# Perceiver block on one core: key rows by SBUF-to-SBUF transfers, batch 0 prepared alone, squarings moved, and key scores and exponential per head

## Chip, cores and metric

One core of a Trainium2 chip runs the whole program in one launch. The metric is device microseconds of that core, median of three runs. All matrix data are float32 or, where the text says so, bfloat16 (bf16).

## What is computed

The reference is one Perceiver layer on x (4 batches, 128 tokens, 128 features) and a context of 2048 rows per batch; attention has 16 heads of 8 features:

```python
q = (layernorm(x) @ Wq.T + bq);  k = ctx @ Wk.T + bk;  v = ctx @ Wv.T + bv      # per head: 8 columns
attn = softmax(q @ k.T / sqrt(8) + mask)                                        # 128 x 2048 per head
x = x + (attn @ v) @ Wo.T + bo
sigma = svd(W)[0];  W_in, W_out = W / max(sigma, 1)                             # largest singular values
x = x + gated_scan(layernorm(x), W_in, W_out, Wp, ...)                          # 128 steps
x = x + (gelu(layernorm(x) @ bw1.T + b1) @ bw2.T + b2)                          # bw: alpha * sign(w)
```

## The kernel before

**Units.** Attention runs over 4 batches x 8 pairs of heads x 4 chunks of 512 keys = 128 units. For each unit TensorE makes three products. `scores` (L418) is queries x keys, 128 x 512 for each head of the pair, in bf16: the two heads lie in partitions 0 to 63 and 64 to 127 of `k_rows`, so each of the two matmuls uses one half of the array's rows. VectorE takes the row maximum of it (`pmax`, L1191). Then `keyscores` (L434) makes the same product the other way round, keys x queries, with the maximum subtracted: 8 matmuls of 128 keys x 128 queries, four for each head, and in the kernel before the heads alternate (j outside, head inside). ScalarE takes the exponential of both heads in one instruction (`probs`, L739), and `pv` (L447) multiplies with the values, 16 float32 passes onto four column groups.

**Splitting.** A float32 query or key is held as three bf16 parts; the contraction of a head is over 8 features x 6 products of parts = 48 rows, plus 3 rows for the maximum in `keyscores`.

**Key rows.** The three parts lie feature by feature in `k_parts`. To get the 48 rows of a head, SP stores each chunk to DRAM (`store_k`, L259, three DMAs of 384, 256 and 128 KB) and loads two blocks of 192 KB for each pair (`load_pair`, L267) into one of four slots of `k_rows`. Queries go the same way, once (`q_rows_dram`, L282 and L288). GpSimd copies the query block and the value block of each pair (`q_now` L982, `v_now` L959).

**Order.** Chunks 0 to 7 (batches 0 and 1) are turned, projected and split before attention starts. Then the loop over g = 0 to 127 issues on TensorE, in this order, `keyscores(g + 1)`, `scores(g + 8)`, `pv(g)` and one piece of side work:

```python
keyscores(g + 1); scores(g + LEAD); pv(g)        # LEAD = 8
if g < 64:    side_prep(8 + g // 8, g % 8, i)    # one of chunks 8 to 15 per 8 units
elif g < 112: side_squares(g, i)                 # 3 squarings per 8 units
else:         side_last(g, i)
```

Of 8 units in `side_prep` one turns the context chunk (L320), two project halves of K (L487), two halves of V (L495), two (g % 4 == 1) turn the running output and the next maximum (`side_turns`, L455 and L460), and one has no side work. The largest singular values come from 24 squarings of a Gram matrix: six lie in the preparation, 18 in `side_squares`. All waits are on semaphores written by hand: `keyscores(g + 1)` waits for the exponential of g, the exponential of g + 1 for `keyscores(g + 1)`, since there is one pair of PSUM banks (4 and 5) for it; `scores(u)` waits for the maximum of u - 2. `side_prep(8, 0)` waits for context chunk 8. TensorE, ScalarE, VectorE, GpSimd and SP's queue each execute in the order of the program.

Of the kernel before, what the change touches and what calls it, by code (L numbers as in the profile page):

```python
# [43 lines left out]
def perceiver_block(nc, x, ctx_in, mask, Wq, bq, Wk, bk, Wv, bv, Wo, bo, W_in, W_out, Wp, bp,  # L44
# [25 lines left out]
    HALF_ROWS = 64  # L70
    LOADS = 32
# [4 lines left out]
    with ctx:  # L76
# [41 lines left out]
        q_now = sb("q_now", [P, 4, T], BF16)  # L118
        ctx_buf = sb("ctx_buf", [P, FIRST, 4, D])
        ctxT = sb("ctxT", [P, 2, 512])  # L120
        k_parts = sb("k_parts", [P, 3, B * KEYS], BF16)
        k_r1 = sb("k_r1", [P, 2, 512])
        k_32 = sb("k_32", [P, 2, 512])
# [3 lines left out]
        v_now = sb("v_now", [P, 2, KT, 2 * HEAD_COLS])  # L127
# [8 lines left out]
        o_nat = w1_nat  # L136
# [26 lines left out]

        q_dram = nc.dram_tensor("q_rows_dram", (D, BLOCKS, TOK), BF16, kind="Internal").ap()
        k_dram = nc.dram_tensor("k_rows_dram", (B, D, BLOCKS, KEYS), BF16, kind="Internal").ap()

        ld = {n: sem("ld_" + n) for n in ("ident", "x", "kv", "vec_qk", "vec", "ssm", "w", "mlp",
                                          "mask", "rows")}  # L170
        ctx_loaded = [sem(f"ctx_loaded{c}") for c in range(FIRST)]
# [14 lines left out]
        k_stored_first = sem("k_stored_first")  # L186
        k_stored_rest = sem("k_stored_rest")
        q_now_ready = sem("q_now_ready")
        k_rows_loaded = [sem(f"k_rows_loaded{s}") for s in range(4)]
        v_now_ready = sem("v_now_ready")  # L190
# [40 lines left out]

        @block.sync
        def _(sp):
            def load_ctx(n):
                wait(sp, ctx_turned, n - FIRST + 1)
                b, c = divmod(n, CHUNKS)
                sp.dma_start(ctx_buf[:, n % FIRST, :, :], ctx_in[b, 512 * c:512 * c + 512, :].rearrange(
                    "(p j) d -> p j d", j=4)).then_inc(ctx_loaded[n % FIRST], 16)

            sp.dma_start(w_kv[:, 0, :], Wk).then_inc(ld["kv"], 16)  # L240
            load_ctx(0)
            sp.dma_start(w_kv[:, 1, :], Wv).then_inc(ld["kv"], 16)
            sp.dma_start(w_kv[:, 2, :], Wq).then_inc(ld["kv"], 16)
            load_ctx(1)
            sp.dma_start(w_nat[:, W_IN, :], W_in).then_inc(ld["ssm"], 16)
            sp.dma_start(w_nat[:, W_OUT, :], W_out).then_inc(ld["ssm"], 16)
            for n in range(2, FIRST):
                load_ctx(n)
            sp.dma_start(mask_sb[:, :], mask.rearrange("a b q k -> (a b q) k")).then_inc(ld["mask"], 16)
            sp.dma_start(w1_nat[:, :, :], w1.rearrange("(a p) d -> p a d", p=P)).then_inc(ld["mlp"], 16)  # L250
            sp.dma_start(w2_nat[:, :], w2).then_inc(ld["mlp"], 16)


            def store_k(n):
                b, c = divmod(n, CHUNKS)
                sp.wait_ge(k3_ready, n + 1)
                keys = slice(512 * c, 512 * c + 512)
                for first, parts in K_GROUPS:
                    sp.dma_start(k_dram[b, :, first:first + parts, keys],  # L259
                                 k_parts[:, 0:parts, 512 * n:512 * n + 512]  # L260
                                 ).then_inc(k_stored_rest if b else k_stored_first, 16)

            def load_pair(i):
                b, p = divmod(i, PAIRS)
                wait(sp, keyscores_ready, CHUNKS * (i - 3))
                for h in range(2):
                    sp.dma_start(k_rows[HALF_ROWS * h:HALF_ROWS * h + ROWS, i % 4, :],  # L267
                                 k_dram[b, 16 * p + HD * h:16 * p + HD * h + HD, :, :].rearrange("r i n -> (r i) n")
                                 ).then_inc(k_rows_loaded[i % 4], 16)

            def small_vectors():
                for v, at in ((bv, BV), (alpha_log, ALPHA), (delta_bias, DBIAS), (bp, BP0), (b1, B1_0)):
                    n = v.shape[0] // P
                    sp.dma_start(vec_nat[at:at + n, :], v.rearrange("(a p) -> a p", p=P)).then_inc(ld["vec"], 16)
                sp.dma_start(w_nat[:, W_O, :], Wo).then_inc(ld["w"], 16)
                sp.dma_start(w_nat[:, W_P:W_P + 3, :], Wp.rearrange("(a p) d -> p a d", p=P)).then_inc(ld["w"], 16)

            store_k(0)
            store_k(1)
            sp.wait_ge(once("q_parts_ready"), 1)  # L280
            for first, n, part in ((0, 3, 0), (3, 2, 1), (5, 1, 2)):
                sp.dma_start(q_dram[:, first:first + n, :], q_parts[:, part:part + 1, :].broadcast_to((P, n, TOK))  # L282
                             ).then_inc(once("q_stored"), 16)
            store_k(2)
            sp.wait_ge(once("q_stored"), 16 * 3)
            sp.wait_ge(once("q_all_zeroed"), 1)
            for h in range(2):
                sp.dma_start(q_all[HALF_ROWS * h:HALF_ROWS * h + ROWS, :, :, :].rearrange("r p b t -> r p (b t)"),  # L288
                             q_dram.rearrange("(p h r) i n -> h (r i) p n", p=PAIRS, h=2)[h]
                             ).then_inc(once("q_loaded"), 16)  # L290
            store_k(3)
            sp.wait_ge(once("k_ones_ready"), 1)
            sp.wait_ge(k_stored_first, 16 * len(K_GROUPS) * CHUNKS)
            for i in range(4):
                load_pair(i)
            for n in range(CHUNKS, FIRST):
                store_k(n)
            small_vectors()
            for n in range(FIRST, ALL_CHUNKS):
                load_ctx(n)  # L300
            for i in range(4, ALL_PAIRS):
                if i % PAIRS == 0:
                    sp.wait_ge(k_stored_rest, 16 * len(K_GROUPS) * CHUNKS * (i // PAIRS))
                load_pair(i)
                if i >= 6 and i % 2 == 0 and FIRST + i // 2 - 3 < ALL_CHUNKS:
                    store_k(FIRST + i // 2 - 3)
# [9 lines left out]
        def _(pe):  # L316
# [6 lines left out]
            pe.wait_ge(ld["kv"], 48)  # L323
            for i in range(3):
                turn(ps[:, 1, P * i:P * i + P], w_kv[:, i, :])
            pe.wait_ge(ld["vec_qk"], 32)
            pe.transpose(ps[:, 1, 3 * P:3 * P + 2], vec_nat[0:2, :], ident[0:2, 0:2]).then_inc(once("kv_turned"), 1)


            def turn_ctx(bank, n):  # L330
                pe.wait_ge(ctx_loaded[n % FIRST], 16 * (n // FIRST) + 16)
                for j in range(4):
                    t = turn(ps[:, bank, P * j:P * j + P], ctx_buf[:, n % FIRST, j, :])
                t.then_inc(ctx_turned, 1)

            def project_k(n):
                pe.wait_ge(ctxT_ready, n + 1)
                wait(pe, k1_ready, n - 1)
                wait(pe, r1_ready, n - 1)
                pe.matmul(ps[:, 2 + n % 2, :], kvT[:, 0, :], ctxT[:, n % 2, :], start=True, stop=True  # L340
                          ).then_inc(k_done, 1)

            def project_v(n):
                wait(pe, v_ready, n - 1)
                for j in range(4):
                    t = pe.matmul(ps[:, 4 + n % 2, P * j:P * j + P], ctxT[:, n % 2, P * j:P * j + P], kvT[:, 1, :],
                                  start=True, stop=True)
                t.then_inc(v_done, 1)

            def sum_norms(norms):  # L350
                pe.wait_ge(fro_ready, 2 * norms + 2)
                pe.matmul(ps[:, 7, 0:2], ones[:, :], fro[:, :], start=True, stop=True).then_inc(fro_summed, 1)

            def square(bank, k):
                pe.wait_ge(pow_ready, k + 1)
                for w in range(2):
                    t = pe.matmul(ps[:, bank, P * w:P * w + P], power[:, k % 2, w, :], power[:, k % 2, w, :],  # L357
                                  start=True, stop=True)
                t.then_inc(sq_done, 1)

            pe.wait_ge(once("kvT_ready"), 1)
            for n in range(FIRST):
                wait(pe, ctxT_ready, n)
# [14 lines left out]
                if n >= 1:  # L378
                    project_v(n - 1)
# [1034 lines left out]
```

## Time and profile before

| | |
|---|---|
| median of 3 runs | 327.06 us (324.84 to 327.69) |
| profiled execution | 329.18 us, of which 327.4 us are the span of the trace |
| busy: TensorE, VectorE, ScalarE, GpSimd | 257.0, 231.3, 200.7, 108.2 us |
| first `scores`, first exponential | 48.1 and 56.9 us |
| context chunk 8 turned (`side_prep(8, 0)`) | 64.0 us |
| end of the last `pv` | 276.8 us |
| mean granted clock of TensorE | 0.895 of full speed |

The loop takes two thirds of the span, the preparation a sixth, and what follows attention (projections, gates, scan, MLP) the last 50 us.

### The profile page before, as it was taken

To read this page: it belongs to the slowest core of one execution; us is meant where nothing else is said; L and a number is where in the kernel's file an instruction comes from. 1 tells how busy PE (TensorE), PEld (TensorE's weight loads), DVE (VectorE), ACT (ScalarE), POOL (GpSimd) and SP (SyncE) were. 2 spreads that over 40 slices of the span, in tenths; PEclk is the share of its full clock that TensorE was granted. 3 is DMA by queue.
4 is the path that set the end of the run, shared out by engine and by line. 5 is a ranking of instruction groups with operands and counts; after the bars stand their busy time and mean duration, and the time that the engine had idled before them with its cause. 6 is when DMAs were issued, how large, how long until landed. Compare 5 with 4: busy or idle time off the path is not lost.

```text
span 327.4 us, 9590 instructions
## 1 busy us (share of the span) xinstructions
PE 257.0 (79%) x3904; PEld 160.6 (49%) x3904; DVE 231.3 (71%) x425; ACT 200.7 (61%) x309; POOL 108.2 (33%) x267
## 2 busy tenths in 40 slices
PE   0799615499999999999999999999999877550276
PEld 0577401245555556555565655555655444440156
DVE  4358839267878788787878989879888940538941
ACT  1267700267777777877777777777876665195042
POOL 7123421115434553345433665232113120104210
PEclk9999955569999999999999999999999996785559
DMA  6926979941535415344263312311321000000001
GB/s 146 381 88 220 226 179 292 363 153 50 148 92 153 146 50 161 107 127 145 52 188 102 103 50 77 73 50 50 80 68 52 3 4 2 0 0 0 0 0 32
DMA packets 24565, 34.48 MB, mean 105 GB/s; under 512 B 2444, under 2 KB 19112, under 8 KB 24392
## 3 DMA queue, kind: packets, MB, share of 16 engines
q1 hardware_dynamic: 23716, 33.37, 35.0%
q8 instruction: 33, 0.54, 0.7%
q0 software_dynamic: 128, 0.14, 0.5%
q10 hardware_dynamic: 676, 0.33, 0.3%
q14 instruction: 12, 0.10, 0.1%
HBM read 20.20 MB, written 13.63 MB: 103 GB/s over the span
## 4 chain that ended last, share of the span: by engine, by line
PE 58%; ACT 17%; SPq 6%; DMA 6%; DVE 6%; issue 5%; POOL 2%; POOLq 0%; ACTq 0%; DVEq 0%
PE ps L447 15%; ACT probs L739 13%; PE ps L434 13%; PE ps L418 6%; PE ps L320 4%; PE ps L357 4%; SPq L259 4%; PE ps L487 3%; PE ps L495 3%; DMA k_rows_dram<-k_parts 2%; DMA w_kv<-in_L_xattn_Wq_dram 2%; PE ps L455 2%; PE ps L667 2%; PE ps L340 2%; DMA ctx_buf<-in_ctx_dram 1%
## 5 line engine op out<-in xcount | busy, mean ns | idle before, releaser
L1191 DVE TENSOR_REDUCE pmax<-ps 128x2 f32<-128x1024 f32 x128 | 156.1, 1224 | 42.8 <-PE ps L418 41.0
L739 ACT ACTIVATE probs<-ps 128x1024 f32<-128x1024 f32 x128 | 130.8, 1022 | 47.2 <-PE ps L434 47.2
L447 PE MATMUL ps<-probs,v_now 128*9 128x128 f32 x2048 | 82.4, 280 | 0.2 <-ACT probs L739 0.2
L434 PE MATMUL ps<-q_max,k_rows 51*128 51x128 bf16 x1024 | 52.3, 223 | 13.9 <-ACT probs L739 12.8
L447 PEld LDWEIGHTS ps<-probs,v_now 128*9 128x9 f32 x2048 | 43.8, 91 | 34.9 <-issue 33.1
L418 PE MATMUL ps<-k_rows,q_now 48*128 48x512 bf16 x256 | 51.2, 398 | 11.0 <-DMA k_rows<-k_rows_dram 8.3
L968 POOL CAST max_cols<-negmax 128x2 bf16<-128x2 f32 x32 | 6.1, 192 | 133.6 <-DVE negmax L1197 133.6
L434 PEld LDWEIGHTS ps<-q_max,k_rows 51*128 51x128 bf16 x1024 | 30.0, 96 | 37.5 <-ACT probs L739 22.7
L418 PEld LDWEIGHTS ps<-k_rows,q_now 48*128 48x128 bf16 x256 | 12.8, 96 | 14.2 <-DMA k_rows<-k_rows_dram 8.5
L690 ACT ACTIVATE ctxT<-ps 128x512 f32<-128x512 f32 x16 | 9.6, 597 | 14.2 <-PE ps L320 14.2
L357 PE MATMUL ps<-power 128*128 128x128 f32 x96 | 16.7, 297 | 0.2 <-DVE power L1119 0.2
L634 PE MATMUL ps<-wT,q_r 128*128 128x128 f32 x8 | 2.4, 461 | 18.0 <-DVE q_r L1348 18.0
L900 POOL TENSOR_TENSOR k_parts<-k_r,k_parts 128x512 bf16<-128x512 f32 x8 | 9.3, 1157 | 20.9 <-ACT k_parts L690 20.9
L320 PE MATMUL ps<-ident,ctx_buf 128*128 128x128 f32 x64 | 11.5, 308 | 5.3 <-DMA ctx_buf<-in_ctx_dram 4.0
L357 PEld LDWEIGHTS ps<-power 128*128 128x128 f32 x96 | 12.5, 190 | 4.3 <-issue 3.0
L690 ACT ACTIVATE v_all<-ps 128x256 f32<-128x256 f32 (+1 forms) x24 | 10.9, 454 | 5.9 <-PE ps L495 5.9
L455 PEld LDWEIGHTS ps<-gather,oT_sb 128*128 128x128 f32 x64 | 9.9, 195 | 8.0 <-issue 7.7
L455 PE MATMUL ps<-gather,oT_sb 128*128 128x18 f32 x64 | 13.1, 281 | 0.5 <-ACT oT_sb L690 0.5
L959 POOL COPY v_now<-v_all 128x288 f32<-128x288 f32 x32 | 13.5, 422 | 0.0
L690 ACT ACTIVATE xnT<-ps 128x256 f32<-128x256 f32 (+1 forms) x5 | 2.1, 425 | 18.2 <-PE ps L320 18.2
L1211 DVE COPY o_raw<-ps 128x18 f32<-128x18 f32 x32 | 5.3, 166 | 10.2 <-PE ps L455 10.2
L320 PEld LDWEIGHTS ps<-ident,ctx_buf 128*128 128x128 f32 x64 | 7.9, 155 | 8.3 <-issue 6.5
(184 smaller groups left out, 360.0 us busy)
## 6 DMA issues: line engine op xcount, KB each, us to landing
k_rows<-k_rows_dram SPq DMA_DIRECT2D x64, 192.0 KB, 3.3
k_rows_dram<-k_parts SPq DMA_DIRECT2D x16, 384.0 KB, 3.8
ctx_buf<-in_ctx_dram SPq DMA_DIRECT2D x16, 256.0 KB, 5.5
k_rows_dram<-k_parts SPq DMA_DIRECT2D x16, 256.0 KB, 3.7
k_rows_dram<-k_parts SPq DMA_DIRECT2D x16, 128.0 KB, 4.1
mask_sb<-in_mask_1x1xSxS_ff_dram SPq DMA_DIRECT2D x1, 1024.0 KB, 9.3
q_all<-q_rows_dram SPq DMA_DIRECT2D x2, 384.0 KB, 6.5
w_nat<-in_L_ffn_w_dram SPq DMA_DIRECT2D x2, 256.0 KB, 8.8
```

The lines of the kernel that those rows point to most:

```text
L259: sp.dma_start(k_dram[b, :, first:first + parts, keys], k_parts[:, 0:parts, 512 * n:512 * n + 512]).then_inc(k_stored_rest if b else k_sto ...
L320: return pe.transpose(dst, src, ident[:, :])
L357: t = pe.matmul(ps[:, bank, P * w:P * w + P], power[:, k % 2, w, :], power[:, k % 2, w, :], start=True, stop=True)
L418: t = pe.matmul(ps[:, bank + h, :], q_now[rows, i % 4, :], k_rows[rows, i % 4, 512 * c:512 * c + 512], start=not masked, stop=True)
L434: t = pe.matmul(dst, k_rows[rows, i % 4, at:at + P], q_max[rows, i % 2, :], start=not masked, stop=True, skip_group_check=masked)
L447: t = pe.matmul(ps[at:at + HEAD_COLS, 6, 0:P], v_now[:, i % 2, 4 * c + j, HEAD_COLS * h:HEAD_COLS * h + HEAD_COLS], probs[:, c, h, P * j:P ...
L455: return pe.matmul(ps[:, 7, 384:384 + 2 * HEAD_COLS], oT_sb[:, i % 2, :], gather[:, :], start=True, stop=True)
L487: pe.matmul(ps[:, 7, half], kvT[:, 0, :], ctxT[:, n % 2, half], start=True, stop=True).then_inc(k_done, 1)
L690: act.activation(dst, src, ACT.Copy).then_inc(s, n)
L739: act.activation(probs[:, u % CHUNKS, :, :], ps[:, 4:6, :], ACT.Exp).then_inc(probs_ready, 1)
L959: gp.tensor_copy(v_now[:, i % 2, :, :], v_all[:, KT * b:KT * b + KT, 2 * HEAD_COLS * p:2 * HEAD_COLS * (p + 1)]).then_inc(v_now_ready, 1)
L1191: dve.tensor_reduce(pmax[:, i % 2, :, c], ps[:, bank:bank + 2, :], AX.X, ALU.max).then_inc(pmax_ready, 1)
```

## The change

1. **Key rows from SBUF to SBUF.** `store_k`, `k_dram`, `q_now` and `v_now` go. Each pair is loaded by six DMAs straight out of `k_parts`, with seven products of parts (56 rows) instead of six; queries still pass through DRAM, batch 0 first and batches 1 to 3 later. `scores` reads `q_all` and `pv` reads `v_all` directly.
2. **Batch 0 alone first.** Chunks 0 to 3 are prepared, then attention starts; chunks 5 to 7 and the projection of the other queries lie between the first `scores`.
3. **Squarings** are all in units 64 to 112, four per 8 units instead of three, normalised every fourth; the turning of weights is spread over the groups.
4. **Per head.** `keyscores` does the four matmuls of head 0, then the four of head 1; the exponential is two instructions of 512 columns.

The core of the diff:

```diff
 def keyscores(u, masked):
-    wait(pe, probs_ready, u)
-    for j in range(4):
-        for h in range(2):
+    for h in range(2):
+        wait(pe, probs_ready, 2 * u - 1 + h)
+        for j in range(4):
             ...
-    t.then_inc(keyscores_ready, 1)
+        t.then_inc(keyscores_ready, 1)
 def exp_unit(u):
-    act.wait_ge(keyscores_ready, u + 1)
     wait(act, pv_done, u - 3)
-    act.activation(probs[:, u % CHUNKS, :, :], ps[:, 4:6, :], ACT.Exp).then_inc(probs_ready, 1)
+    for h in range(2):
+        act.wait_ge(keyscores_ready, 2 * u + h + 1)
+        act.activation(probs[:, u % CHUNKS, h, :], ps[:, 4 + h, :], ACT.Exp).then_inc(probs_ready, 1)
+def load_half_pair(eng, i, h):
+    for rows, parts in ((slice(at, at + TRIPLE), PARTS), (slice(at + TRIPLE, at + 2 * TRIPLE), PARTS),
+                        (slice(at + 2 * TRIPLE, at + ROWS), 1)):
+        eng.dma_start(k_rows[rows, slot, :], k_parts[heads, 0:parts, keys]).then_inc(k_rows_loaded[slot], 16)
 # SP
+    load_ctx(0); Wk; load_ctx(1..3); Wv; mask; load_ctx(4, 5)
+    sp.wait_ge(once("q_parts_ready"), 1); store_q(sp, first_tokens); load_ctx(6, 7)
+    sp.wait_ge(once("q_stored"), 16 * 3); load_q(batch 0)          # 6 DMAs
+    sp.wait_ge(k3_ready, EARLY); load_half_pair(sp, 0, 0)          # ACT issues half 1
+    load_pair(1..3); w1; w2                                        # 18 + 2 DMAs
+    sp.wait_ge(once("q_parts_ready"), 2); store_q(sp, rest_tokens); W_in; W_out
+    sp.wait_ge(once("q_stored"), 32 * 3); load_q(batches 1 to 3)   # 6 DMAs
+    load_ctx(FIRST)                                                # chunk 8
+    ...
 # TensorE
+def early_chunk(n):
+    pe.wait_ge(ctxT_ready, n);         turn_ctx(7, n)
+    pe.wait_ge(k32_ready, n - EARLY);  project_k(6, n)
+    wait(pe, v_ready, n - 1);          project_v(4 + n % 2, n)
 def attend(masked):
+    scores(0); scores(1); <project batches 1 to 3 of q>; scores(2)
+    pe.wait_ge(once("q_step"), 5)
+    early_chunk(5); scores(3); early_chunk(6); scores(4); early_chunk(7); scores(5)
 # GpSimd
+third(0); third(1); rest_root(); third(2); third(3)      # rest_root waits for xn_var 2
 # VectorE
+layernorm((0,), 0); rest_k(0..2); split_q_first; rest_k(3); split_q; split_q_rest
+mask_magnitude(0); mask_magnitude(1); layernorm((1, 2, 3), 1)    # this gives xn_var 2
+# after the maximum of unit 3: split_q(rest_tokens); of unit 4: split_q_rest(rest_tokens) -> q_parts_ready 2
 def side_squares(g, i):
-    k = EARLY_SQUARES + SQ_PERIOD * m       # at 0, 2, 4
+    k = SQ_PERIOD * m                       # at 0, 2, 3, 4; weights turned at 6 for m in 0, 1, 3, 4
```

`whole_k` and `split_k` now also take chunks 4 to 7; the weight means and signs of the MLP move on VectorE from the preparation to after units 42 and 44.

## Rows read from the trace of the kernel before

**Rows 1.** The page: chain that ended last, by engine.

```profile
PE 58%; ACT 17%; SPq 6%; DMA 6%; DVE 6%; issue 5%; POOL 2%; POOLq 0%; ACTq 0%; DVEq 0%
```

**Rows 2.** Timeline of TensorE in two units: start us, us, instructions.

```profile
150.86 0.40 PE L434 MATMUL ps<-q_max,k_rows 51*128 51x128 bf16 x8
151.09 0.38 PE L418 MATMUL ps<-k_rows,q_now 48*128 48x512 bf16 x2
...
151.96 0.70 PE L487 MATMUL ps<-ctxT,kvT 128*128 128x256 f32 x2
...
152.59 0.40 PE L434 MATMUL ps<-q_max,k_rows 51*128 51x128 bf16 x8
...
155.43 0.40 PE L455 MATMUL ps<-gather,oT_sb 128*128 128x18 f32 x2
...
155.85 0.40 PE L434 MATMUL ps<-q_max,k_rows 51*128 51x128 bf16 x8
```

**Rows 3.** The same keyscores group, answers for the first 40 and 90 ns.

```profile
150.86 0.23 PE L434 MATMUL ps<-q_max,k_rows 51*128 51x128 bf16 x2
...
150.86 0.29 PE L434 MATMUL ps<-q_max,k_rows 51*128 51x128 bf16 x4
```

**Rows 4.** Timeline of two units without side work, near the loop's end.

```profile
264.29 0.40 PE L434 MATMUL ps<-q_max,k_rows 51*128 51x128 bf16 x8 [0.34 <-ACT probs L739]
...
264.73 1.02 ACT L739 ACTIVATE probs<-ps 128x1024 f32<-128x1024 f32 x1 [0.33 <-PE ps L434]
...
265.81 0.40 PE L434 MATMUL ps<-q_max,k_rows 51*128 51x128 bf16 x8 [0.56 <-ACT probs L739]
...
266.14 0.62 PE L447 MATMUL ps<-probs,v_now 128*9 128x128 f32 x16
```

**Rows 5.** Timeline of ScalarE: two copies of 512 columns, one behind the other.

```profile
21.32 0.60 ACT L690 ACTIVATE ctxT<-ps 128x512 f32<-128x512 f32 x1 [0.62 <-PE ps L320]
...
21.81 0.59 ACT L690 ACTIVATE xnT<-ps 128x512 f32<-128x512 f32 x1
```

**Rows 6.** Chain in order of time: the same place of two neighbouring groups of 8 units.

```profile
107.85 1.03 ACT probs L739
...
121.25 1.03 ACT probs L739
```

**Rows 7.** Side work of units 64 (chain) and 112, last pv (timeline).

```profile
173.69 0.66 PE ps L357 x4
...
252.75 0.71 PE L570 MATMUL ps<-power,gram 128*128 128x128 f32 x4
...
275.74 1.04 PE L447 MATMUL ps<-probs,v_now 128*9 128x128 f32 x16 [0.15 <-ACT probs L739]
```

**Rows 8.** Timeline of the preparation, all engines.

```profile
10.77 1.12 PE L320 MATMUL ps<-ident,ctx_buf 128*128 128x128 f32 x4 [0.64 <-ACT vec L690]
...
13.48 1.91 PE L340 MATMUL ps<-ctxT,kvT 128*128 128x512 f32 x2
...
27.34 1.16 POOL L900 TENSOR_TENSOR k_parts<-k_r,k_parts 128x512 bf16<-128x512 f32 x1 [2.12 <-ACT k_parts L690]
...
29.54 1.56 SPq L282 DMA_DIRECT2D q_rows_dram<-q_parts  x3
...
33.50 1.17 SPq L288 DMA_DIRECT2D q_all<-q_rows_dram  x2
...
36.11 2.33 DVE L1078 TENSOR_REDUCE mask_abs<-mask_sb 128x1 f32<-128x1024 f32 x2
...
43.48 3.99 SPq L267 DMA_DIRECT2D k_rows<-k_rows_dram  x8
...
48.08 1.03 PE L418 MATMUL ps<-k_rows,q_now 48*128 48x512 bf16 x4 [8.25 <-DMA k_rows<-k_rows_dram]
```

**Rows 9.** The stall for context chunk 8, timeline.

```profile
59.48 3.94 SPq L237 DMA_DIRECT2D ctx_buf<-in_ctx_dram  x8
...
64.02 1.09 PE L320 MATMUL ps<-ident,ctx_buf 128*128 128x128 f32 x4 [3.99 <-DMA ctx_buf<-in_ctx_dram]
```

More of the change, by code:

```diff
@@ L241, in _ @@
             load_ctx(0)
[L242 to L247, printed above, removed]
+            sp.dma_start(w_kv[:, 0, :], Wk).then_inc(ld["wk"], 16)
+            for n in range(1, EARLY):
                 load_ctx(n)
+            sp.dma_start(w_kv[:, 1, :], Wv).then_inc(ld["wv"], 16)
@@ L249, in _ @@
             sp.dma_start(mask_sb[:, :], mask.rearrange("a b q k -> (a b q) k")).then_inc(ld["mask"], 16)
[L250 to L261, printed above, removed]
+            for n in range(EARLY, CTX_SLOTS):
+                load_ctx(n)
@@ L279, in _ @@
-            store_k(1)
+                    load_half_pair(sp, i, h)
+            first_tokens, rest_tokens = slice(0, T), slice(T, TOK)
             sp.wait_ge(once("q_parts_ready"), 1)
[L281 to L284, printed above, removed]
+            store_q(sp, first_tokens)
@@ L285, in _ @@
+            for n in range(CTX_SLOTS, FIRST):
+                load_ctx(n)
             sp.wait_ge(once("q_stored"), 16 * 3)
@@ L320, in turn @@
                 return pe.transpose(dst, src, ident[:, :])
[L323 to L327, printed above, removed]
             def turn_ctx(bank, n):
-                pe.wait_ge(ctx_loaded[n % FIRST], 16 * (n // FIRST) + 16)
+                pe.wait_ge(ctx_loaded[n % CTX_SLOTS], 16 * (n // CTX_SLOTS) + 16)
@@ L388, in _, with turn_xn @@
-            project_k(FIRST - 1)
-            project_v(FIRST - 1)
-            sum_norms(EARLY_SQUARES // SQ_PERIOD)
-            pe.wait_ge(once("q_step"), 1)
-            pe.wait_ge(once("mask_abs_ready"), 1)
-            turn(ps[0:1, 1, 0:P], mask_abs[:, 0:1]).then_inc(once("mask_turned"), 1)
+            def turn_xn(first, n):
+                for i in range(first, first + n):
+                    t = turn(ps[:, 3, P * i:P * i + P], xn[:, i, :])
+                t.then_inc(once("xn_turned"), 1)
@@ L728, in _ @@
[L728 to L732 removed]
+                copy(v_heads(4 * n, 4), ps[:, bank, :].rearrange("p (t m) -> p t m", m=HD), v_ready)
+            copy_ctx(0, 0)
+            act.wait_ge(once("k_turned"), 1)
+            copy(kvT[:, 0, :], ps[:, 2, 0:P], once("vec_ready"))
+            copy(vec[:, 0:2], ps[:, 2, 3 * P:3 * P + 2], once("kT_ready"))
+            copy_ctx(1, 1)
@@ new lines, in _ @@
+            first_k(0)
+            copy_ctx(0, 2)
+            first_k(1)
+            copy_ctx(1, 3)
+            first_k(2)
+            act.wait_ge(once("qv_turned"), 1)
+            copy(kvT[:, 2, :], ps[:, 2, P:2 * P], once("vec_ready"))
+            copy(kvT[:, 1, :], ps[:, 2, 2 * P:3 * P], once("qT_ready"))
+            act.wait_ge(once("xn_turned"), 1)
+            copy(xnT[:, 0:T], ps[:, 3, 0:T], once("qT_ready"))
+            first_k(3)
+            for n in range(EARLY):
+                take_vall(6 + n % 2, n)
@@ L733, in _ @@
+            act.wait_ge(once("k_ones_ready"), 1)
+            act.wait_ge(k3_ready, EARLY)
+            load_half_pair(act, 0, 1)
+            act.wait_ge(once("xn_turned"), 2)
+            copy(xnT[:, T:TOK], ps[:, 3, T:TOK], once("qT_ready"))
+            for n in range(EARLY, FIRST):
+                copy_ctx(7, n)
+                whole_k(n)
+                take_vall(4 + n % 2, n)
             act.wait_ge(ld["rows"], 16 * 4)
```

622 lines of the change are left out of this document (321 added, 301 removed).

## The prediction

> **What bounds the kernel now.** I read the chain that ended last first: TensorE holds 58% of it and ScalarE 17% [rows 1], so the question is where the loop goes from one to the other. The timeline of TensorE in a unit with heavy side work answers it [rows 2]: keyscores start at 150.86, scores at 151.09, the side work (half of a K projection) at 151.96, the next keyscores at 152.59. Nothing stands between them. This unit costs 1.73 us and is all TensorE: 0.23 for keyscores, 0.87 for scores and pv, 0.63 for side work. A unit with `side_turns` has 0.42 there (155.43 to 155.85), so 1.10 + 0.42 = 1.52. A unit without side work would be 1.10, but takes 1.52 as well [rows 4]: 264.29 to 265.81, with TensorE idle until the exponential of 1.02 us is done. That is the other loop, keyscores to exponential to keyscores: 0.44 from the start of keyscores to the start of the exponential (264.29 to 264.73), 1.02 of exponential, 0.06 back. So of 8 units of `side_prep` five are bound by TensorE, two by both equally and one by the chain through ScalarE. Together they take 121.25 - 107.85 = 13.40 us [rows 6]; my parts give 8 x 1.10 + 5 x 0.63 + 2 x 0.42 + 0.42 = 13.2.
>
> The preparation ends with two waits for transfers: the first scores start at 48.08 [rows 8], and context chunk 8 is turned only at 64.0, after 4 us of waiting, since SP issues its load at 59.48 [rows 9].
>
> **Part 4, per head.** The exponential becomes two of 512 columns. Two copies of that size start 0.49 apart and last 0.60 [rows 5], so the pair costs 1.09 instead of 1.02 and head 0's keyscores can run beneath head 1's exponential: the chain through ScalarE falls from 1.52 to about 1.1 per unit. That is worth something only where the chain binds: one unit in 8 of `side_prep`.
>
> What it costs is in the answers for 40 and 90 ns [rows 3]. After 40 ns two matmuls of the eight have started, after 90 ns four; they end at 0.23 and 0.29, and all eight at 0.40 [rows 2]. So two run at a time, one for each head in its half of the array's rows, and a pair costs 0.057 us. In the new order the first four all belong to head 0: each must follow the one before in the same half, and head 1's are behind them in the queue. Eight steps of 0.057 are 0.46 instead of 0.23. Where the halves meet (head 0's last beside head 1's first, head 1's last beside the first scores) one step overlaps, so scores start at about 0.40 and **TensorE pays 0.17 us more in each unit**. Bounds: 0 (the engine starts head 1 early all the same) and 0.29 (no overlap, 0.23, and one more step of 0.057 for the wait ahead of head 1). I take 0.17, because they show both halves at work only where instructions for both stand next to each other.
>
> Here a rule of the Trainium skill speaks against the change. *TensorEngine Tiling (Array Packing)*, section Key Properties, says that different tiles can execute weight loads and matmuls in parallel; *TensorE: Matmul & The Clock Gate*, section Step-by-step, says that matmuls stay in program order and only weight loads are pulled ahead. By the first alone the order would not matter; by both the new order serialises, as taken here.
>
> `side_prep`: each group pays 8 x 0.17 = 1.36, and gets back 0.42 in the unit that the chain had bound (VectorE's maximum, started once a unit, would hold that unit at about 1.25, TensorE at 1.27). Net +0.94, times 8 groups: **+7.5 us**, and about +0.5 more since the first group runs at the half clock.
>
> **Part 3, squarings.** From the first squaring in the loop at 173.69 to the Rayleigh product at 252.75 are 79.1 us [rows 7] for 48 units with 18 squarings. After: each group is 8 x 1.27 + 4 x 0.65 (a squaring is 0.66) [rows 7] + 2 x 0.42 + 0.4 for the sum of norms = 14.0; six are 84.0, weight turning in four groups adds 2.2, the last sum of norms is missing (-0.4): 85.8. The spaces that the chain left in these units (three of 8 had little side work) are what the old kernel used for nothing and the new one fills. **+6.7 us**. The squarings taken out of the preparation lay beside transfers there, so they free little. The new waits (a square needs ScalarE's copy from the unit before) are met: that copy starts when the square and the exponentials of its unit are done, over 0.6 us before TensorE asks.
>
> **Last 16 units**, 252.75 to 276.8 (275.74 + 1.04): 24.1 us [rows 7]. The first 8 are bound by VectorE and TensorE alike, 12.1 after. The last 8 have no scores: keyscores 0.33 (265.81 to 266.14) [rows 4] + 0.17 + pv 0.55 = 1.05 each and 0.84 for turns, 9.3, and I add 1.3 for the half clock at the very end. Sum 22.7: **-1.4 us**. Loop in all: +7.5 + 0.5 + 6.7 - 1.4 = **+13.3**.
>
> **Part 2, the preparation.** Four chunks instead of eight, and the first turn need not wait for all three weights: I put it at 4 us instead of 10.8. TensorE's work for K of four chunks is, at its durations [rows 8], two times (1.12 + 1.91) cold and two times about 1.6 warm, 9.3 us; with the splitting behind it and q of batch 0 that makes 14, so query parts are ready at 18. But GpSimd's `rest_root` stands ahead of `third(2)` and waits for the layernorm of batches 1 to 3, which VectorE does behind the mask's maximum: 18 + 2.3 (mask) + 2 = 22.4, then three GpSimd operations of about 1.16 (27.34) [rows 8]: the keys are complete at 25.9. The half pair behind it costs 3 x 0.5 of issue (8 took 3.99) and 3.6 to land (second of the eight issued by 44.5, scores at 48.08), 31; the four small loads that GpSimd now issues behind `third(3)` and that attention waits for come in at about 33. **First scores at 33 instead of 48.1.**
>
> That gain is then mostly given back. Three chunks, the rest of q and six scores stand in a row on TensorE: first about 3.5 us for two scores and the q projection, then each early chunk is turn, ScalarE's copy, K, V, one after the other: 1.1 + 0.8 + 1.9 + 1.6 cold, 3.2 warm. `scores(4)` is at 45.5. Behind its maximum VectorE finishes the other query parts, 48.2. **SP waits for these before chunk 8**: store 1.6 (29.54), 2.6 to land (31.1 to 33.50 is 2.4) [rows 8], six loads of 0.58 (two took 1.17), 3.5, then the load of chunk 8, issued by 56.3, and 4.1 to land (59.9 to 64.02) [rows 9]: `side_prep(8, 0)` at 60.4 instead of 64.0. **-3.6 us.** Bounds: -14 (the early chunks overlap better and scores start by 28) and +3 (each step cold, small loads slow). The start of scores alone, 15 us earlier, is not the gain; the first unit that waits for chunk 8 is.
>
> **Part 1, key rows.** Six issues of 0.5 for a pair are 3.0 us of SP, then 3.6 to land: 6.6, against six units (10.7 us) between the wait for the freed slot and `scores`. Hidden, as are the store DMAs and GpSimd's copies that go. If a load lands over 4 us later than that, every pair stalls.
>
> **Sum.** +13.3 - 3.6 = +9.7 on the profiled execution of 329.2 gives 338.9; that one lies 2.1 above the median of 327.06, so **337 us**.
>
> **Rivals.** *A, no serialisation*: head 1's matmuls run beside head 0's, 0 instead of 0.17. For it: the two heads lie in separate halves of the rows. (It is what the Trainium skill's Key Properties of *TensorEngine Tiling (Array Packing)* would give by itself.) Against: each pair of matmuls waits for the pair before [rows 3]. Then `side_prep` groups are 13.0 (-3), squarings 8 x 1.10 + 3.84 = 12.6 to 13.2 a group (about -1), the end -3, with the preparation -10.6: 318.6, median **317**. It decides from below 0.08 us a unit, half of my price. This is the way to the other side. *B, the preparation gains in full*: chunk 8 is turned at 52 instead of 60. For it: 15 us are really gained at the first scores. Against: the place of `load_ctx(FIRST)` in SP's queue. 338.9 - 8.4 = 330.5, median **328**. *C, the key loads arrive late*, 8 source partitions feeding each: 1 us for each of 28 pairs would give **365**; the slack of 4 us above speaks against it.
>
> **How the numbers follow.** Forecast 60%, A 14%, B 20%, C 6%. A range from 323 to 346 leaves out most of A and C and holds the unknown prices: 0.17 can be 0.23 (+6) and the preparation can move by 10. A measurement can tell about 1% (3.3 us) from no change. Faster by over 1%: A and a third of B, 0.20. Within 1%: the rest of B and the lower edge of the forecast, 0.16. Slower: 0.64.
>
> **What the new profile would show.** Keyscores' start to scores' start 0.40 instead of 0.23 where TensorE does not wait; groups of `side_prep` at 14.3 and of squarings at 14.0 to 14.7; TensorE without idle time in the loop, ScalarE idle more; in the last 8 units about 1.2 instead of 1.5; first scores near 33, `third(2)` after 22, chunk 8 turned near 60 after a wait for its DMA. The forecast is wrong if scores follow keyscores after 0.23, if chunk 8 comes before 55, or if `scores` waits for `k_rows` inside the loop.

## Result and the profile after

The changed kernel takes 370.1 us (four runs, 365.1 to 372.4) against 326.1 us: ratio 1.130, 95% interval 1.116 to 1.143. The forecast was 337 us, its range 323 to 346. The time of the profiled execution is 370.12 us, its span 368.3 us, so 40.9 us more span than before. A profiled execution isn't the median (329.2 us against 326.1 before, 331.3 against 329.0 in e5, 321.2 against 319.9 in e10), so differences of spans below are good to a few us.

The page of the changed kernel, part 4 (the chain that ended last, by engine and by line) and two rows of part 6 (DMA issues):

```profile
SPq 46%; PE 23%; DMA 10%; DVE 9%; issue 4%; POOL 3%; ACT 3%; POOLq 0%; DVEq 0%; ACTq 0%
SPq L232 43%; DMA k_rows<-k_parts 7%; PE ps L451 6%; PE ps L434 4%; DMA ctx_buf<-in_ctx_dram 3%; PE ps L418 2%; PE ps L322 2%; PE ps L704 2%; DVE pmax L1209 2%; PE ps L460 1%; SPq L255 1%; PE ps L495 1%; PE ps L712 1%; DMA q_last_dram<-q_parts 1%; PE ps L333 1%
...
k_rows<-k_parts SPq DMA_DIRECT2D x126, 96.0 KB
...
k_rows<-k_parts SPq DMA_DIRECT2D x63, 32.0 KB
```

Where TensorE held 58% of the chain [rows 1], SP's queue now holds 46%, and 43% are one line: L232, the issue of the key loads. A queue of issues as the bound means that the transfers behind it can't keep up or that there are too many of them; the experiments decide which. The timeline of SP and TensorE in the loop (start us, us, instructions, idle time before and what ended it; the time of a merged row runs from its first start to its last end, pauses included):

```profile
86.79 14.74 SPq L232 DMA_DIRECT2D k_rows<-k_parts  x12
101.57 1.89 SPq L255 DMA_DIRECT2D ctx_buf<-in_ctx_dram  x1
...
189.53 17.92 SPq L232 DMA_DIRECT2D k_rows<-k_parts  x14
...
192.21 0.41 PE L434 MATMUL ps<-q_max,k_rows 59*128 59x128 bf16 x8
192.45 0.39 PE L418 MATMUL ps<-k_rows,q_all 56*128 56x512 bf16 x2
...
195.09 0.39 PE L418 MATMUL ps<-k_rows,q_all 56*128 56x512 bf16 x2 [0.85 <-DMA k_rows<-k_parts]
...
198.11 0.49 PE L434 MATMUL ps<-q_max,k_rows 59*128 59x128 bf16 x5
198.38 0.39 PE L418 MATMUL ps<-k_rows,q_all 56*128 56x512 bf16 x1
198.43 0.33 PE L434 MATMUL ps<-q_max,k_rows 59*128 59x128 bf16 x3
...
203.02 0.39 PE L418 MATMUL ps<-k_rows,q_all 56*128 56x512 bf16 x2 [0.75 <-DMA k_rows<-k_parts]
```

Fourteen loads take SP 17.92 us, 1.28 each, so the six of a pair take 7.7 us, and SP does nothing else, but that until 137 us it also issues a context chunk (1.89 us at 101.57) for every two pairs. A pair of heads is used up in four units, which were 6.7 us before (half of 13.40). `scores` waits for its keys again and again: every pair now costs 8.2 us in `side_prep` and 8.0 in the squarings. Over the whole kernel the waits are (engine and line, what was waited for: total us, times, longest):

```profile
PEld ps L418 <- DMA k_rows<-k_parts: 25.1, 21, 2.1
PE ps L418 <- DMA k_rows<-k_parts: 19.6, 19, 1.9
PE ps L322 <- DMA ctx_buf<-in_ctx_dram: 10.5, 2, 10.2
```

Places of the loop, as the start of `pv` of units 0, 8, 64, 112 and 127, from TensorE's timeline, with kernels of the experiments below beside the two (profiled executions, us):

| | 0 | 8 | 64 | 112 | 127 | span |
|---|---|---|---|---|---|---|
| before | 59.0 | 79.2 | 173.1 | 252.2 | 275.7 | 327.4 |
| after | 54.9 | 80.7 | 195.4 | 291.1 | 317.3 | 368.3 |
| e5_sixteen_engines | 56.3 | 76.5 | 175.8 | 257.1 | 278.5 | 329.5 |
| e10_version | 55.4 | 71.0 | 167.3 | 248.7 | 270.0 | 319.4 |

Differences of neighbouring columns give the budget of the 40.9 us: +1.5 up to unit 8, +20.8 in units 8 to 64, +16.6 in 64 to 112, +2.7 to the last unit, -0.7 behind it. The loss is spread evenly over units 8 to 112, 1.4 us a pair, and isn't a matter of their side work. It goes on while `scores` still run (units 112 to 120 take 16.3 us, 12.4 before) and ends with them.

The preparation after, the same view (part of it), answers [rows 8, 9]:

```profile
19.87 0.86 POOL L944 TENSOR_TENSOR rstd<-var_eps,neg_half 128x3 f32<-128x3 f32 x1 [6.38 <-DVE var_eps L1074]
20.70 2.25 POOL L952 TENSOR_TENSOR k_parts<-k_r,k_parts 128x512 bf16<-128x512 f32 x2
...
23.03 27.44 SPq L232 DMA_DIRECT2D k_rows<-k_parts  x21
23.05 4.64 ACTq L232 DMA_DIRECT2D k_rows<-k_parts  x3
...
33.80 0.61 PE L418 MATMUL ps<-k_rows,q_all 56*128 56x512 bf16 x4 [1.19 <-issue]
...
48.65 0.85 DVE L1103 TENSOR_TENSOR q_parts<-q_r,q_parts 128x384 bf16<-128x384 f32 x1
...
53.15 1.25 SPq L236 DMA_DIRECT2D q_wide_dram<-q_parts  x2
...
60.34 0.83 SPq L255 DMA_DIRECT2D ctx_buf<-in_ctx_dram  x2
...
66.09 1.09 PE L322 MATMUL ps<-ident,ctx_buf 128*128 128x128 f32 x4 [10.19 <-DMA ctx_buf<-in_ctx_dram]
```

Scores start 14 us earlier than before, and chunk 8 is turned 2 us later: 21 key loads hold SP until 50.5, and everything behind them in its queue moves back.

### The profile page after: what moved, and what is told of

Read it like the earlier page. It is cut to its first block, busy times and chain, and to the rows that moved or that the text cites. A ratio compares the mean times of both kernels' runs of the same rounds, so it can differ in the third digit from the quotient of the medians.

```text
span 368.3 us, 9729 instructions
## 1 busy us (share of the span) xinstructions
PE 284.7 (77%) x3902; PEld 177.9 (48%) x3902; DVE 228.3 (62%) x409; ACT 210.3 (57%) x440; POOL 98.6 (27%) x216
## 4 chain that ended last, share of the span: by engine, by line
SPq 46%; PE 23%; DMA 10%; DVE 9%; issue 4%; POOL 3%; ACT 3%; POOLq 0%; DVEq 0%; ACTq 0%
SPq L232 43%; DMA k_rows<-k_parts 7%; PE ps L451 6%; PE ps L434 4%; DMA ctx_buf<-in_ctx_dram 3%; PE ps L418 2%; PE ps L322 2%; PE ps L704 2%; DVE pmax L1209 2%; PE ps L460 1%; SPq L255 1%; PE ps L495 1%; PE ps L712 1%; DMA q_last_dram<-q_parts 1%; PE ps L333 1%
## 5 line engine op out<-in xcount | busy, mean ns | idle before, releaser
L786 ACT ACTIVATE probs<-ps 128x512 f32<-128x512 f32 x256 | 139.0, 595 | 27.3 <-PE ps L434 26.1
L451 PE MATMUL ps<-probs,v_all 128*9 128x128 f32 x2048 | 85.6, 288 | 0.7 <-ACT probs L786 0.7
L418 PE MATMUL ps<-k_rows,q_all 56*128 56x512 bf16 x256 | 57.7, 406 | 23.8 <-DMA k_rows<-k_parts 19.6
L434 PE MATMUL ps<-q_max,k_rows 59*128 59x128 bf16 x1024 | 65.5, 228 | 1.6 <-ACT probs L786 0.9
L451 PEld LDWEIGHTS ps<-probs,v_all 128*9 128x9 f32 x2048 | 44.6, 92 | 37.6 <-issue 34.1
L434 PEld LDWEIGHTS ps<-q_max,k_rows 59*128 59x128 bf16 x1024 | 39.5, 98 | 25.5 <-ACT probs L786 9.1
L418 PEld LDWEIGHTS ps<-k_rows,q_all 56*128 56x128 bf16 x256 | 16.1, 99 | 29.1 <-DMA k_rows<-k_parts 25.1
L333 PE MATMUL ps<-ctxT,kvT 128*128 128x512 f32 x16 | 11.4, 801 | 6.1 <-ACT ctxT L729 6.1
L970 POOL TENSOR_TENSOR k_parts<-k_r,k_parts 128x512 bf16<-128x512 f32 x12 | 14.1, 1176 | 1.0
L964 POOL TENSOR_TENSOR k_r<-k,k_parts 128x512 f32<-128x512 f32 x12 | 13.9, 1155 | 1.0
```

The lines of the kernel that those rows point to most:

```text
L333: pe.matmul(ps[:, bank, :], kvT[:, 0, :], ctxT[:, n % EARLY, :], start=True, stop=True).then_inc(k_done, 1)
L418: t = pe.matmul(ps[:, bank + h, :], q_all[rows, i % PAIRS, i // PAIRS, :], k_rows[rows, i % 4, 512 * c:512 * c + 512], start=not masked, s ...
L434: t = pe.matmul(dst, k_rows[rows, i % 4, at:at + P], q_max[rows, i % 2, :], start=not masked, stop=True, skip_group_check=masked)
L451: t = pe.matmul(ps[at:at + HEAD_COLS, 6, 0:P], v_all[:, KT * (i // PAIRS) + 4 * c + j, first + HEAD_COLS * h: first + HEAD_COLS * h + HEAD ...
L786: act.activation(probs[:, u % CHUNKS, h, :], ps[:, 4 + h, :], ACT.Exp).then_inc(probs_ready, 1)
L970: gp.tensor_tensor(k_parts[:, 2, keys], r1, k_parts[:, 1, keys], ALU.subtract).then_inc(k3_ready, 1)
```

## Experiments

### Part 4 alone: e1_order_only and e2_per_head_only

Both start from the kernel before. e1 takes only the order of `keyscores`, e2 the whole of part 4 (two waits, two exponentials).

```diff
-                for j in range(4):
-                    for h in range(2):
+                for h in range(2):
+                    for j in range(4):
```

Expected of e1:

> The kernel before with one edit: keyscores does head 0's four matmuls, then head 1's four; one wait and one exponential as before. My prediction's theory (row halves serialise, 0.17 us a unit, 0.42 us given back nowhere): units bound by TensorE pay in full, about +16 to +20 us, 342 to 346. The rival that the new profile suggests (scores follow keyscores after 0.23 to 0.24 there too, so the halves overlap in any order): within 1% of 326.

Expected of e2:

> The kernel before with part 4 whole: keyscores and exponential per head, nothing else. My prediction's theory: about +10 us (the serialised halves, less the freed chain through ScalarE). The rival (halves overlap in any order): only units without side work gain, 1 in 8 of side_prep, some 3 in 8 of the squarings and the last 16, together 5 to 12 us faster: 314 to 321.

Measured: e1 327.96 us, ratio 1.0054 (1.0023 to 1.0084); e2 328.04 us, 1.0048 (1.0014 to 1.0083), both within the 1% that I count as no change, though the intervals put both a little above the kernel before. e1 is where the rival put it; e2 is where neither expectation put it (+10 us, or 314 to 321). A group of `side_prep` is 13.51 us in e1 and 13.70 in e2 against 13.40 [rows 6]. So the order costs 0.11 us in 8 units, 0.014 a unit and not 0.17. The timeline of TensorE in e1 shows it, scores 0.24 behind keyscores where it was 0.23 [rows 2]:

```profile
151.07 0.41 PE L434 MATMUL ps<-q_max,k_rows 51*128 51x128 bf16 x8
151.31 0.39 PE L418 MATMUL ps<-k_rows,q_now 48*128 48x512 bf16 x2
```

The changed kernel shows why, in the rows at 198.11 to 198.43 above: `scores` of head 0 starts 0.05 us before the last three `keyscores` of head 1, which stand ahead of it in the program. Matmuls for different halves of the array's rows didn't keep the program's order, so what stands ahead of the prediction, that TensorE executes in the order of the program, doesn't hold here across the two halves. In e1's trace two `keyscores` have started 30 ns after the first and four after 100 ns, as in [rows 3], although the four of one head now stand behind those of the other:

```profile
151.07 0.24 PE L434 MATMUL ps<-q_max,k_rows 51*128 51x128 bf16 x2
...
151.07 0.30 PE L434 MATMUL ps<-q_max,k_rows 51*128 51x128 bf16 x4
```

The forecast drew on *TensorE: Matmul & The Clock Gate*, section Step-by-step, of the Trainium skill, by which matmuls stay in program order; the rows at 198.38 and 198.43 differ from it, and the measurement decides.

e2's timeline of ScalarE and TensorE in a unit with light side work shows what the split exponential brings:

```profile
159.72 0.39 ACT L690 ACTIVATE v_all<-ps 128x256 f32<-128x256 f32 x1 [0.40 <-PE ps L495]
160.11 1.08 ACT L740 ACTIVATE probs<-ps 128x512 f32<-128x512 f32 x2
160.17 0.62 PE L447 MATMUL ps<-probs,v_now 128*9 128x128 f32 x16
160.76 0.77 PE L434 MATMUL ps<-q_max,k_rows 51*128 51x128 bf16 x6
...
161.35 0.37 PE L418 MATMUL ps<-k_rows,q_now 48*128 48x512 bf16 x1
161.37 0.27 PE L434 MATMUL ps<-q_max,k_rows 51*128 51x128 bf16 x2
...
161.79 0.62 PE L447 MATMUL ps<-probs,v_now 128*9 128x128 f32 x16
```

ScalarE's copy of the values comes first, then both exponentials; head 1's keyscores wait for the second, which ends at 161.19 (the answer for the time up to 161.2 has four matmuls of the eight, the one up to 161.3 has five), and the unit takes 161.79 - 160.17 = 1.62 us, not the 1.1 that the forecast gave this chain, nor less than the 1.52 before. Where no such copies stand ahead, the split does pay: in the last seven units e2 takes 9.2 us and the kernel before 11.1.

### The key loads: e4_half_bytes, e5_sixteen_engines, e9_dram_source

All three start from the changed kernel. e4 loads only the first 1024 of 2048 keys of each row from pair 4 on, in the same number of DMAs (`scores` and `keyscores` of chunks 2 and 3 of a batch then use old keys; nothing else is left out):

```diff
+                n = KEYS // 2 if i >= 4 else KEYS
-                eng.dma_start(k_rows[rows, slot, :], k_parts[heads, 0:parts, keys])
+                eng.dma_start(k_rows[rows, slot, 0:n], k_parts[heads, 0:parts, KEYS * b:KEYS * b + n])
```

> The changed kernel, but from pair 4 on each of the six key loads of a pair brings only the first 1024 of 2048 keys (the others stay from an earlier pair, so attention is computed with wrong keys): same number of issues, half the bytes and packets of 2 KB. Theory D (the 8 DMA engines that serve these loads are full, 14 packets of about 0.53 us for each engine and pair = 7.4 of the 8.0 us that a pair takes, and SP's issues only wait for room): loads stop setting the pace, 320 to 335. Theory I (an issue of this kind costs SP about 1.28 us whatever it moves, six a pair = 7.7 us): no change, 365 to 372.

e5 changes the layout: row 8 x feature + product instead of 24 rows after 24, so that one DMA takes one product of all 16 partitions of a pair. That makes seven loads of 64 KB instead of six of 96 and 32; bytes stay the same. Queries follow the layout (three stores, seven loads).

```diff
-            for rows, parts in (...):                              # 8 source partitions each
-                eng.dma_start(k_rows[rows, slot, :], k_parts[heads, 0:parts, keys])
+            for row in (range(0, 4) if h == 0 else range(4, 7)):   # 16 source partitions each
+                eng.dma_start(k_rows[row:P:8, slot, :], k_parts[16 * p:16 * p + 16, row % PARTS, keys])
```

> The changed kernel with the key rows laid out so that one load moves one product of parts for 16 features of both heads (partitions 8 apart): 7 loads of 64 KB a pair with 16 source and 16 target partitions instead of 6 loads with 8 source partitions; bytes unchanged. Theory D: 16 DMA engines share the packets, 7 for each, about 4 us a pair, so the loads are hidden: 315 to 330. Theory I: 7 issues of 1.28 us are 9.0 us a pair, slower than now: 395 to 405.

e9 keeps the six loads and their targets but reads them, from pair 4 on, from rows of 4 KB of the mask in DRAM (attention of these pairs is then over zeros instead of keys):

```diff
+                if i >= 4:
+                    src = mask.rearrange("a b q k -> (a b q) k")[0:HD * parts, 0:KEYS // 2].bitcast(BF16)
```

> The changed kernel, but from pair 4 on the six key loads of a pair read rows of zeros of the mask in DRAM instead of k_parts (attention over wrong keys): same shapes, 8 x 3 rows of 4 KB, same targets, same 8 engines. If SBUF as the source makes a 4-KB packet 0.53 to 0.62 us instead of 0.23: 14 packets are 3.5 us for each engine and pair, the loads are hidden, 330 to 338. If 8 engines with these targets are slow by themselves: packets stay over 0.5 us, 362 to 372.

| | us | ratio to before | packet, median us | q1 share |
|---|---|---|---|---|
| before | - | 1 | 0.23 | 23.8% |
| after | 370.12 | 1.130 | 0.62 | 47.5% |
| e4, 2-KB packets | 335.45 | 1.0275 (1.0221 to 1.0329) | 0.30 | 28.9% |
| e5 | 329.04 | 1.0093 (1.0050 to 1.0136) | 0.36 | 41.6% |
| e9 | 335.85 | 1.0297 (1.0214 to 1.0381) | 0.16 | 24.0% |

Packet durations are from the packet records: of the 4-KB packets of each trace, in e9 of those from 210 to 230 us (before pair 4 its loads are those of the changed kernel), in e4 of the 2-KB packets in that window. The share is that of SP's queue in the window from 210 to 230 us; a row has packets, MB and busy share of the 16 DMA engines. After:

```profile
q1 hardware_dynamic: 397, 1.14, 47.5%
```

e5, same window:

```profile
q1 hardware_dynamic: 666, 1.36, 41.6%
...
k_rows<-k_parts SPq DMA_DIRECT2D x22, 64.0 KB, 2.4
```

The 47.5% is 95% of eight engines. The packet records say the same: in that window 7 or 8 packets were in flight during 89% of the time in the changed kernel, while the kernel before goes to 16 and above and e5 to 14. Each of eight engines carries 14 packets a pair (56 rows x 2 heads / 8) of 0.53 us on average: 7.4 us of the 8 that a pair takes. The engines themselves aren't named in the records; eight is read from the packets in flight. It agrees with a rule of the Trainium skill (*DMA: Bandwidth & Descriptors*, section Why a DMA increments its semaphore by 16 and not by 1), by which a transfer uses the largest number of engines, at most 16, that divides the slowest dimension of both sides: 8 source partitions give eight.

SP's time per issue isn't a constant of the instruction. Timelines of SP: e5 in the preparation, where it is 18.02 / 25 = 0.72 us,

```profile
24.50 18.02 SPq L228 DMA_DIRECT2D k_rows<-k_parts  x25
```

e5 and e9 in the loop, the seven and the six of a pair, 0.61 and 0.36 each,

```profile
206.61 4.29 SPq L228 DMA_DIRECT2D k_rows<-k_parts  x7
...
210.86 2.14 SPq L238 DMA_DIRECT2D k_rows<-in_mask_1x1xSxS_ff_dram  x6
```

0.71 in e4 (six in 4.26), and 1.28 in the changed kernel. What SP itself waits for from 80 to 290 us, the `keyscores` that free a slot of `k_rows` (total us, times, longest), in the changed kernel and in e5:

```profile
SPq L208 <- PE ps L434: 3.4, 3, 1.3
...
SPq L206 <- PE ps L424: 55.3, 25, 5.5
```

In e4 that wait is 65.5 us in all and in e9 119.0. So in the changed kernel SP hardly ever waits for TensorE, in the other three before nearly every pair: there the loads no longer set the pace. e4 has the changed kernel's issues one for one, and each takes little more than half as long. So the price of an issue isn't fixed, as theory I had it; it follows what the transfers have to move.

So any of the three, fewer bytes, sixteen engines or another source, takes 34 to 41 us away, and no wait for `k_rows` is left in the loop. (e4 ends half a microsecond above its expected range. It and e9 keep the full loads of the first four pairs, and with them the changed preparation: unit 8 comes at 82.4 and 80.6, in e5 at 76.5. That is most of what e5 is ahead of them.) e5 alone shows that the access pattern is enough, since its source is still SBUF and its bytes are the same. It doubles the engines and the SBUF partitions of a load together, and its packets are faster too; no run takes sixteen engines with 8 partitions, so which of the two did it isn't shown. e9 isn't as clean as it was meant to be: its records most often show 12 packets in flight while it loads, so it changed the engines as well as the source. Whether the source alone would have done it, and how much of 0.62 against 0.23 us a packet is the source and how much the crowding on eight engines, stays open. At sixteen engines each, SBUF to SBUF took 0.36 and DRAM to SBUF 0.23.

### What is left: e6_joint_again, e7_weights_spread, e8_chunk8_first

These start from e5. e6 undoes part 4 in it. e7 takes the weight means and signs, which the change put on VectorE in two blocks after units 42 and 44, as single instructions after units 42, 43, 46, 47, 50, 51 and 54. e8 takes the load of chunk 8 ahead of SP's wait for the other queries.

```diff
 # e6
-                for h in range(2):
-                    wait(pe, probs_ready, 2 * u - 1 + h)
-                    for j in range(4):
+                wait(pe, probs_ready, u)
+                for j in range(4):
+                    for h in range(2):
 # e7
-                elif u == 42:
-                    weight_means()
-                elif u == 44:
-                    weight_signs()
+                elif u in (42, 43, 46, 47, 50, 51, 54):
+                    weight_step((42, 43, 46, 47, 50, 51, 54).index(u))
 # e8
+            load_ctx(FIRST)
+            load_ctx(FIRST + 1)
             sp.wait_ge(once("q_parts_ready"), 2)
```

> The sixteen-engine kernel with part 4 undone (heads alternate in keyscores, one exponential of 1024 columns). What part 4 alone cost in the kernel before was 13.70 instead of 13.40 us per group of side_prep, 0.5% in all. If that adds up here too: 2 to 3 us faster than the sixteen-engine kernel, 326 to 327. If per-head work pays once the squarings are denser (the rival, the change's idea): 2 to 5 us slower than it, 331 to 334.

> The sixteen-engine kernel with the weight means and signs not in two lumps on VectorE after units 42 and 44 but one instruction each after units 42, 43, 46, 47, 50, 51 and 54. One group of eight units takes 17.0 us there instead of 13.7, with TensorE waiting 2.0 us for VectorE's copy: if the lump is the cause, 3 us faster, 326, and that group back at 13.7. If the stall has another cause (the start of batch 1): no change.

> The sixteen-engine kernel with context chunks 8 and 9 loaded by SP ahead of its wait for the other query parts, not behind the six or seven query loads. If the order in SP's queue is what holds side_prep(8, 0), as I predicted, it starts at 57.3 instead of 62.3: 4 to 7 us faster, 322 to 325. If something else comes late right behind it (the four key slots, SP's later loads): under 2 us faster.

Measured: e6 329.39 us, ratio 1.0069 (1.0032 to 1.0106), not to be told from e5's 1.0093, and between the two expectations. The traces say why: groups of `side_prep` are 13.51 us against 13.70 in e5, but the last 15 units take 23.6 instead of 21.3. Part 4 loses in the one place what it gains in the other.

e7 326.04 us, 0.9954 (0.9910 to 0.9997). In e5 the group of g = 32 to 39, in which the maxima of units 40 to 47 are made (`scores` leads by 8), lasts 17.0 us, in e7 13.97. VectorE's and TensorE's timelines of e5 there:

```profile
126.48 0.83 DVE L1111 TENSOR_SCALAR k_parts<-w_nat 128x512 f32<-128x512 f32 x1
127.23 1.38 DVE L1112 TENSOR_SCALAR k_parts<-w_nat 128x512 f32<-128x512 f32 x1
128.53 0.41 DVE L1111 TENSOR_SCALAR k_parts<-w_nat 128x512 f32<-128x512 f32 x1
128.87 0.41 DVE L1112 TENSOR_SCALAR k_parts<-w_nat 128x512 f32<-128x512 f32 x1
...
130.53 0.16 DVE L1220 COPY o_raw<-ps 128x18 f32<-128x18 f32 x1
...
130.76 1.20 PE L493 MATMUL ps<-kvT,ctxT 128*128 128x128 f32 x4 [1.98 <-DVE o_raw L1220]
```

The maximum of each unit stands behind the block, `scores` behind the maximum, and TensorE 1.98 us behind a copy of VectorE. The first two instructions take 0.83 and 1.38 us, the same two afterwards 0.41 each: GpSimd's work on `k_parts` (126.42 to 128.33) overlaps the first two and not the others. In e7 none of the four overlaps GpSimd and each takes 0.42, so e7 gains by that as well as by the spreading; how much by which wasn't measured. In the changed kernel this was hidden behind the key loads.

e8 324.60 us, 0.9908 (0.9861 to 0.9954). Chunk 8 in e5, on the timelines of SP and TensorE:

```profile
59.00 1.06 SPq L245 DMA_DIRECT2D ctx_buf<-in_ctx_dram  x2
...
62.31 1.09 PE L312 MATMUL ps<-ident,ctx_buf 128*128 128x128 f32 x4 [4.98 <-DMA ctx_buf<-in_ctx_dram]
```

and in e8, without a wait:

```profile
56.75 1.12 PE L312 MATMUL ps<-ident,ctx_buf 128*128 128x128 f32 x4
```

Unit 8's `pv` comes 4.9 us earlier (71.6 instead of 76.5). The two executions are alike up to there (chunk 7 turned at 48.3 and 48.6), so this gain is the edit's. The granted clock is at its lower level for 3.4 us in e8 (0.5 of full speed from 55.8 to 59.2) and for 10.2 in e5 (55.7 to 66.0), where TensorE stood still for 5 us.

### Together: e10_version and e11_version_joint

e10 is e5 with both edits, e11 the same with part 4 undone.

> The sixteen-engine kernel with both repairs: weights spread on VectorE and chunks 8 and 9 loaded ahead of the wait. If the two savings measured one by one (about 4 and 6 us) add: 318 to 321, 2 to 3% faster than the kernel before. If the later arrival of batch 2 or of the queries eats one: 322 to 325.

> The same with part 4 undone as well (heads alternate, one exponential). Part 4 was worth nothing either way with the sixteen-engine loads: within 0.5% of the version per head, 317 to 322.

e10 319.93 us, ratio 0.9741 (0.9690 to 0.9792); e11 320.54 us, 0.9773 (0.9732 to 0.9814). Both are faster than either given kernel; e10's interval lies wholly beyond 2% below the kernel before, e11's reaches across it. The page of e10 has TensorE at the head of the chain again:

```profile
PE 68%; DVE 10%; ACT 5%; issue 5%; SPq 4%; DMA 3%; POOL 2%; ACTq 1%; POOLq 0%; DVEq 0%
```

and a window of its loop (busy us and count of PE, PEld, DVE, ACT, POOL, granted clock, DMA share, GB/s) has no idle time on TensorE:

```profile
215.00:235.00 20.00, 20.00 (x349) 13.11 (x347) 17.04 (x32) 16.35 (x35) 3.39 (x15) 1.00 0.41 68
```

where the changed kernel, at the same granted clock, has:

```profile
200.00:220.00 20.00, 16.92 (x286) 10.75 (x288) 13.24 (x24) 14.29 (x31) 6.99 (x17) 1.00 0.48 59
```

Part 4 was tried in three surroundings, with it and without: 1.0048 (1.0014 to 1.0083) against 1 in the kernel before, 1.0093 against 1.0069, 0.9741 against 0.9773. Alone it costs about half a per cent; in the other two the intervals overlap. In each the traces have the same two effects, 0.2 to 0.3 us more in a group of `side_prep` and 2.2 to 2.3 us less in the last 15 units.

## Why the prediction was wrong

| term | predicted | e5, loads off the path | after |
|---|---|---|---|
| up to unit 8 | -2.2 | -2.7 | +1.5 |
| units 8 to 64 (`side_prep`) | +6.6 | +5.4 | +20.8 |
| squarings | +6.7 | +2.2 | +16.6 |
| last units and tail | -1.4 | -2.8 | +2.0 |
| sum | +9.7 | +2.1 | +40.9 |

(Spans of profiled executions against before. The first group of `side_prep` lies ahead of unit 8, so its share of the forecast, 0.94 + 0.5, stands in the first row with the -3.6 of the preparation. That row is the least certain of the measured ones: unit 8 comes at 79.2, 75.4 and 79.6 in the kernel before, e1 and e2, whose preparation is the same, and at 76.5 and 72.5 in e5 and e7.)

**The step that failed is in "Part 1, key rows": "Six issues of 0.5 for a pair are 3.0 us of SP, then 3.6 to land: 6.6 [...] Hidden".** The 0.5 was the price of an issue while the transfers had room; with eight engines full it was 1.28, and the issue of a pair took 7.7 us against 6.7 us of work. I asked whether one load would land in time and counted its latency against six units of slack. The question was throughput: per pair 14 packets on each of eight engines. Slack in time can't help a queue that falls behind at every pair. At 0.53 us a packet these are 7.4 us; at the 0.23 of the kernel before they would have been 3.2, hidden indeed. So eight engines, which the forecast named in rival C ("8 source partitions feeding each"), and a slower packet, of which no row of before told, came together. Two of the signs that I had named for a wrong forecast are there, `scores` waiting for `k_rows` inside the loop and `scores` 0.24 behind keyscores. **Rival C** had the mechanism and 6% of the chance. Its 365 us come near the measured 370 partly by luck: it had 1 us a pair where 1.4 were lost, on top of a forecast that was about 10 us above the kernel before by costs of which most aren't there.

**Part 4.** The 0.17 us of serialisation isn't there: 0.014 (e1). Rival A had this right. The gain was misjudged too: the chain through ScalarE wasn't 1.1 but 1.62 in a light unit (e2), since copies of the side work stand ahead of the exponentials. In place of 0.94, e2's groups of `side_prep` pay 0.30 each. Rival A had the step right, not the time: it would have had 317, and e2 and e5 stand at 328 and 329. The last units went as forecast: units 112 to 120 take 12.09 us in e2 against 12.42 (forecast 12.1), and those behind them mostly 1.2 to 1.3 each, instead of 1.5.

**The weight means and signs** were named in the change and costed nowhere: 3.3 us of e5's +5.4.

**Part 3, squarings.** +6.7 was forecast, +2.2 measured in e5, and the same in e6, without part 4. The forecast held 48 x 0.17 = 8.2 of serialisation that isn't there; without it my sum would have been -1.5. The 3.7 between lie in the units without a squaring: of units 80 to 87 in e5 the four with one take 1.75 us each, as in my sum, the four others 6.3 together and not 5.6. What holds those four, ScalarE's chain as in e2's light unit, is likely and not shown.

**Part 2, preparation.** Its steps held: first scores at 33.8 (forecast 33), `third(2)` at 20.7 (22.4) and keys complete at 22.95 (25.9), the other query parts at 49.5 (48.2). Then SP's 21 loads of 1.31 instead of 0.5 keep the store of these parts back until 53.15 and put chunk 8 at 66.1 (60.4). In e5, with loads of 0.72, SP is past them at 42.5 and stores the query parts at 51.9, and chunk 8 is at 62.3. So the price of an issue was the larger part of the error here too. That the wait for the queries in front of `load_ctx(FIRST)` and not the start of scores decides, e8 shows.

**Rival B**, 328 us for a preparation gained in full, comes near e5's 329.0, but not by its reason: chunk 8 was turned at 62.3, not at 52.

Had the key loads been off the path, the forecast of +9.7 would have met +2.1 (3 us by the medians). That the changed kernel is slower, as forecast, is luck: the forecast's direction rests on serialisation that doesn't exist and the measured one on key loads that it called hidden.

## What to carry to other kernels

Before a transfer is called hidden, work out its throughput and not its latency alone: packets per engine and use, by a duration per packet, against the work between two uses; and look first how many engines its access pattern reaches. A price of an issue read while the transfers have room is no price of it when they are full. When such a bound is removed, measure the other parts again: a block on VectorE that costs 3.3 us was invisible under it, and a part whose gain and loss cancel can only be judged without it.

## What the runs showed of the hardware

- Loads from 8 partitions of SBUF kept 7 or 8 packets in flight for 89% of a window (q1 at 47.5% of 16 engines), loads from 16 partitions up to 14.
- 4-KB packets took 0.62 us (median) from SBUF in the changed kernel, 0.36 from SBUF in e5, 0.23 from DRAM in the kernel before; 2-KB packets from SBUF in e4 0.30.
- SP's issue of a key load took 1.28 us in the changed kernel, 0.71 with half the bytes (e4), 0.61 to 0.72 in e5 and 0.36 in e9.
- Matmuls for one half of the array's rows started ahead of earlier ones for the other half: 198.38 before 198.43, and 161.35 before 161.37, against the order of the program.
- Eight matmuls of 128 columns, four in each half, had `scores` start behind them after 0.23 us when the halves alternate and after 0.24 when one half's four come first.
- A VectorE TENSOR_SCALAR of 128 x 512 took 0.41 us, and 0.83 and 1.38 while GpSimd worked on SBUF (e5).
